# Stacked keys and values fetched as 120 and 8 partition rows, and w3's last ternary step ahead of two maxima

## What is computed

```python
x = x + xattn0(layernorm(x), ctx, mask)            # softmax(x ctx^T / sqrt(512)) ctx
x = x + ffn0(layernorm(x), w1, w2, w3)             # ternary weights, inputs rounded to 8 bits
x = x + xattn1(layernorm(x), ctx, mask, Wq, Wk, Wv, Wo, ...)   # 16 heads of 32
x = x + ffn1(layernorm(x), integer weights and scales)

def weight_quant(w):                               # w1, w2, w3 of ffn0
    scale = 1.0 / clip(mean(abs(w)), EPS)
    return clip(round(w * scale), -1, 1) / scale
```

## Time and profile before

| | us |
|---|---|
| median of 3 runs | 488.27 (486.84 to 489.53) |
| the profiled execution's own time | 488.89 |
| its span | 487.2 |
| granted TensorE clock over the span | 0.993 |

### The profile page before, as it was taken

How to read it: one execution, slowest core, us unless ns; L and a number is a source line. 1 busy time by engine, 2 the same in 40 slices (tenths; PEclk the granted TensorE clock), 3 DMA queues, 4 the chain that set the end, 5 groups by cost and what they waited for, 6 DMA issues and landing times.

```text
span 487.2 us, 10104 instructions
## 1 busy us (share of the span) xinstructions
PE 467.1 (96%) x3942; PEld 355.4 (73%) x3951; DVE 294.4 (60%) x557; ACT 235.4 (48%) x362; POOL 83.3 (17%) x105
## 2 busy tenths in 40 slices
PE   8999999999999899999999688989999999999997
PEld 6877788777877566676798566878886665556996
DVE  4964464458857887655755323777885976555111
ACT  4655433553576365463846545957755492222000
POOL 2210400005024000001071011232332252000000
PEclk9999999999999999999999988999999999999999
DMA  8999787923694145233397977867323452000111
GB/s 274 352 337 358 288 286 237 314 87 126 229 293 132 54 112 149 70 90 77 104 303 216 267 230 283 245 234 240 110 59 119 131 170 68 1 0 0 39 57 57
DMA packets 59181, 82.75 MB, mean 170 GB/s; under 512 B 20097, under 2 KB 43649, under 8 KB 57985
## 3 DMA queue, kind: packets, MB, share of 16 engines
q1 hardware_dynamic: 59136, 82.14, 53.5%
q10 hardware_dynamic: 2, 0.01, 0.0%
HBM read 58.76 MB, written 14.42 MB: 150 GB/s over the span
## 4 chain that ended last, share of the span: by engine, by line
PE 88%; DVE 7%; issue 3%; DMA 1%; ACT 1%; POOL 0%; DVEq 0%; ACTq 0%
PE psum L1536 14%; PE psum L189 13%; PE psum L187 13%; PE psum L1586 7%; PE psum L1377 6%; PE psum L1339 4%; PE psum L652 4%; PE psum L1444 4%; PE psum L1491 4%; PE psum L1322 4%; PE psum L1386 3%; PE psum L1494 3%; PE psum L1474 3%; PE psum L1503 2%; DVE e L1870 1%
## 5 line engine op out<-in xcount | busy, mean ns | idle before, releaser
L189 PE MATMUL psum<-wv_p,kv_p 128*128 128x512 f32 x288 | 76.2, 413 | 0.0
L187 PE MATMUL psum<-kv_p,wk_p 128*128 128x384 f32 x384 | 74.2, 343 | 0.0
L187 PEld LDWEIGHTS psum<-kv_p,wk_p 128*128 128x128 f32 x384 | 66.8, 188 | 2.1 <-issue 0.2
L189 PEld LDWEIGHTS psum<-wv_p,kv_p 128*128 128x128 f32 x288 | 53.7, 188 | 15.8 <-issue 3.7
L1202 ACT ACTIVATE e<-psum,mask_bias 128x448 f32<-128x448 f32 x96 | 53.9, 637 | 22.7 <-PE psum L1474 22.4
L1870 DVE TENSOR_SCALAR e<-e 128x1344 f32<-128x1344 f32 x32 | 28.8, 900 | 20.1 <-ACT e L1202 20.1
L1491 PE MATMUL psum<-e,vst 128*32 128x112 f32 x768 | 38.2, 270 | 1.6 <-issue 0.9
L1536 PE MATMUL psum<-xt,wg_b 128*128 128x448 f16 x176 | 36.9, 352 | 0.3 <-issue 0.3
L1536 PE MATMUL psum<-xt,wu_b 128*128 128x448 f16 x176 | 36.9, 352 | 0.0
L1586 PE MATMUL psum<-h_p,wd_r 128*128 x176 | 36.7, 369 | 0.0
L209 DVE SCALAR_TENSOR_TENSOR khl<-psum,bqk,khl 128x384 f16<-128x384 f32 x32 | 19.6, 613 | 27.0 <-ACT khl L199 26.8
(11 more groups left out here) (188 smaller groups left out, 815.8 us busy)
## 6 DMA issues: line engine op xcount, KB each, us to landing
kst<-k_scratch SPq DMA_DIRECT2D x32, 384.0 KB, 6.4
kv_raw<-in_ctx_feat SPq DMA_DIRECT2D x12, 768.0 KB, 5.8
w_stage<-in_w SPq DMA_DIRECT2D x6, 1408.0 KB, 8.0
cn<-in_ctx_tok SPq DMA_DIRECT2D x8, 768.0 KB, 9.6
k_scratch<-khl SPq DMA_DIRECT2D x128, 48.0 KB, 1.9
v_scratch<-vsp SPq DMA_DIRECT2D x24, 256.0 KB, 2.8
vst<-v_scratch SPq DMA_DIRECT2D x8, 768.0 KB, 4.6
qst<-qhl SPq DMA_DIRECT2D x32, 112.0 KB, 4.7
```

The lines of the kernel that those rows point to most:

```text
L187: mm = pe.matmul(psum[:, kv_bank(p), 0:TP], wk_p[:, u, k, n * P:(n + 1) * P], src[:, v, k, :], **ends)
L189: mm = pe.matmul(psum[:, kv_bank(p), :], src[:, u, k, n * P:(n + 1) * P], wv_p[:, v, k, :], **ends)
```

## The change

Two things. Each fetch of stacked keys and of stacked values becomes two DMAs on the same queue, one for partitions 0 to 119 and one for 120 to 127, and the two waits count twice as many. Of the source of the keys the slices are 60 and 4 rows, each of which is read twice. Nothing else of SP's order moves. And on DVE `ternary_weight(dve, 2, 1)` and then `hidden(1, 1, 2)` move ahead of the two `largest_input`.

```diff
+        ROWS = ((0, 120), (120, P))
+
         def keys_fetch(sp, b, g):
-            sp.dma_start(kst[b % 2][:, g].rearrange("p h t -> p (h t)"),
-                         k_scratch[b, :, :, g].rearrange("u d h (o t) -> (u d) o (h t)", o=1)
-                         .to_broadcast([2 * HD, 2, 4 * TP])).then_inc(kst_loaded[b % 2], 16)
+            src = k_scratch[b, :, :, g].rearrange("u d h (o t) -> (u d) o (h t)", o=1)
+            for lo, hi in ROWS:
+                sp.dma_start(kst[b % 2][lo:hi, g].rearrange("p h t -> p (h t)"),
+                             src[lo // 2:hi // 2].to_broadcast([(hi - lo) // 2, 2, 4 * TP])).then_inc(kst_loaded[b % 2], 16)

         def values_fetch(sp, b, q):
-            sp.dma_start(vst[q][:], v_scratch[b]).then_inc(vst_loaded[q], 16)
+            for lo, hi in ROWS:
+                sp.dma_start(vst[q][lo:hi], v_scratch[b, lo:hi]).then_inc(vst_loaded[q], 16)
...
-                    pe.wait_ge(kst_loaded[b % 2], 16 * G * (b // 2 + 1))
+                    pe.wait_ge(kst_loaded[b % 2], 16 * G * len(ROWS) * (b // 2 + 1))
...
-                    pe.wait_ge(vst_loaded[b % 2], 16 * (b // 2 + 1))
+                    pe.wait_ge(vst_loaded[b % 2], 16 * len(ROWS) * (b // 2 + 1))
...
             gate_scales(2, 0)
+            ternary_weight(dve, 2, 1)
+            hidden(1, 1, 2)
             largest_input(dve, 5)
             largest_input(dve, 6)
-            hidden(1, 1, 2)
-            ternary_weight(dve, 2, 1)
             input_scales(dve, 1)
```

## The result

The changed kernel takes **508.3 us** (median; 505.7 to 511.3), the kernel before 487.6 (486.1 to 489.5): a ratio of **1.043, 95% interval 1.038 to 1.048**, slower by some 21 us. The forecast was 479.4 with a range of 476.5 to 491, so the sign was wrong and the time lies outside the range. The profiled execution took 507.0 us, its span is 505.3.

The account below looks back on a forecast made before the run. PE, busy 96% of the span, was taken as the bound, its late idle time as waits for its program: 488.9 - 0.85 + 2.1 - 8.5 - 2.3 + 0.6 = 479.9, forecast 479.4 us at the median, range 476.5 to 491.

Parts of the forecast that it names:

- The stalls: Second attention: PE's five waits for its program, 10.3 us, mostly vanish once one engine carries no keys or values; -8.5 us.
- the free engine: Key and value fetches: 120 rows use 15 engines, and the one left out brings PE's program sooner; chance 0.46.
- The clock: Second attention: PE's half-clock stretches after two long stalls mostly go, 2.3 of 2.5 us; -2.3 us.
- SP's issues: Ahead of the attention: 8 more key issues, 5.1 us, make first scores 0.6 late and values 2.1 in all; +2.1 us.
- Fuller engines: Keys of b = 2: a fetch ends with its fullest engine, 10 rows instead of 8, 1.25 us against 1.0; +0.6 us.
- w3: Before down(0): the last ternary step ends 1.71 us earlier, PE's 1.51 us stall goes, part returns at gate_up; -0.85 us.
- Rival 3: Second attention: program fetch shares an engine that gets the 8 rows on top, stalls lengthen, +3.5, 493 us; chance 0.18.

Follow-up runs that it names:

- e12_120_8_late: Kernel before with key and value fetches split at row 120 from the third batch on, the first two batches whole; ratio 1.0211.
- e13_120_8_early: Kernel before with key and value fetches split at row 120 in the first two batches alone, later ones whole; ratio 1.0126.
- e8_120_alone: Kernel before, fetching only rows 0 to 119 of keys and values from the third batch on, with no second transfer; ratio 1.0276.
- e3_96_32: Kernel before with each key and value fetch cut into 96 and 32 rows, DVE's order unchanged; ratio 1.0242.
- e1_w3_only: Kernel before with only the new order on DVE, no fetch split; ratio 0.9985.
- e7_columns: Kernel before with each fetch cut in two along the row (keys by heads, values by chunks), every transfer of 128 rows; ratio 0.9992.
- e9b_paced: Kernel before with SP holding fetches back until earlier ones have landed, no transfer changing its shape; ratio 1.026.

## Why the prediction was wrong

**The step that failed** is in "The stalls": "A transfer of 128 rows can be laid on 16 engines in equal parts of 8 rows, one of 120 rows only on 15", and then a price for rows (ten instead of eight take 1.25 us) that takes a packet's time as given. The layout was right: 94.5% of 16 engines, and 152 packets more than before. By the rule of the Trainium skill, page "DMA: Bandwidth & Descriptors", section "Why a DMA increments its semaphore by 16 and not by 1" (15 engines for 120 rows, 4 and 8 for the 8 rows), there are 32 x (15 + 4 - 16) + 8 x (15 + 8 - 16) = 152 more closing packets, so the measurement agrees with that rule to the packet. What was wrong is that a packet of the same row takes 0.19 us instead of 0.13. That term was in neither the sum nor a rival. Over the 60 us from 280 on it makes 69 us of engine time for a megabyte out of 49, in a stretch where the DMA share was already 0.76. From the third batch on this costs 10 of the 21 us (`e12_120_8_late`); the first two batches, where slow packets and SP's longer issues act together, cost 6 (`e13_120_8_early`).

**The stalls**, predicted at -8.5 us, became longer and more: 23.6 us of "issue" with the first scores' 3.7 in it, against 10.3. What the prediction read them as holds up: each of 20 stalls in three traces ends 1.3 to 1.6 us after a packet of the program, in after they stand 127 or 128 matmuls or twice that apart, and with a bounded queue the first three were 0.7 to 0.8 us. What failed is the step from there to the free engine, that the packet would stand there behind stacks, Wo and integer weights alone: `e8_120_alone` has a free engine, program packets that start as late as in before, and stalls of up to 3.6 us. Whether the packet uses another engine, or waits for something else that a loaded queue delays, no run here tells apart. The prediction also read the DMA share of the stretches as 0.80 to 1.06 from two of the four; the one before the fourth stall (287.89 to 299.97 us) has 0.66.

**The clock**, predicted at -2.3, went the other way as well. After has more stretches at the lower level of 1.2 GHz behind its stalls: of four windows of 3 us, that after the stall of 338.28 has PEclk 0.50, those after 283.7 and 300.1 0.65 and 0.76, and that after 309.7, where PE had stood still for 2.93 us, 1.00. PE's busy time is 5.1 us longer in all.

**SP's issues** were right in kind and half of the size. Predicted: 8 more issues of 0.64, first scores 0.6 late, +2.1 for the values. The queue of SP in after:

```profile
242.41 12.73 SPq L243 DMA_DIRECT2D kst<-k_scratch  x16
255.46 10.32 SPq L544 DMA_DIRECT2D qst<-qhl  x16
265.82 2.60 SPq L248 DMA_DIRECT2D vst<-v_scratch  x4
```

```profile
L243 SPq DMA_DIRECT2D kst<-k_scratch x64: 630/847/1868, 242.4 to 352.4; - x64
```

The key issues take 12.73 us against 6.62, 6.1 more instead of 5.1, and the stacks start 4.2 us later instead of 2.3. The last line (duration in ns, min/median/max) has the cause: one by one, the issues alternate between 0.85 us for 120 rows and 0.63 for 8. In `e3_96_32` the median of the 64 is 598 ns. "0.59 us whether it has 16 or 112 rows" was read from moves of `xres`, and does not hold for 120 rows of keys. To this came slower landing: the last keys and the stacks share the queue, and a stack landed in 3.8 us (2.6 in the earlier trace rows). `e13_120_8_early` prices the whole start at 6.1 us (4.0 to 8.3), three times the term, with slow packets in it.

**Fuller engines**, +0.6, is the term in which most of the loss should have stood. It was worked out from 10 rows in place of 8; that part is not seen, as the 8-row transfers cost nothing that shows in `e12_120_8_late`.

**w3**, -0.85, was right in its mechanism: no idle time stands before `down(0)` in after, and some appears at the next `gate_up`. It gives back 1.1 us in after and 1.3 in `e1_w3_only`, not 0.65, so what is left is 0.2 to 0.4 in PE's waits, and 0.7 with an interval of -0.9 to 2.3 in the time.

**The rivals.** Rival 3 had the sign and named the wrong mechanism; its 493 counts an engine with ten rows, and `e3_96_32`, with all engines even, shows that evenness doesn't help. The rival that was missing is "a transfer that doesn't span 128 rows is slower on every engine". The trace of before had a hint that I did not weigh: the query stacks, written 64 rows at a time, run at a DMA share of 0.72 and 185 GB/s (253.5 to 256 us), 62 us of engine time for a megabyte, where keys of 128 rows take 43 (379 GB/s at 1.015). Their packets are smaller, 1792 bytes. By the same view one takes 0.719 x 16 x 2.5 / 257 = 0.11 us, where the 1536 bytes of `e7_columns` take 0.07, so size is not all of it. But they come from SBUF and not from DRAM, which no run separates.

## What to carry to other kernels

Before a transfer is cut, ask along which axis: cutting it across the partitions made every packet of it slower here, cutting it within the row did not (1.024 to 1.044 against 0.999 for the same number of transfers). In a trace, divide the DMA share by the rate over a loaded stretch; if engine time for a byte rises while the bytes stay, look for a layout and not for a count. And a freed engine is worth nothing before it is known that the waiting work uses it. Where an engine stands still on "issue" within a run of one kind, look for the packet of its program just ahead of the end.

## What was not expected of the hardware

- The same row of 3072 bytes takes an engine 0.13 us in a fetch of 128 rows, 0.19 to 0.20 in fetches of 120, 96/32 or 64/64 rows, and 0.25 when only rows 0 to 63 are written. The mechanism is not shown.
- SP needs 0.60 us to issue a key fetch whether it has 128 rows or 96 and 32, but 0.85 for one of 120 rows.
- 40 more transfers of whole 128-row layout cost nothing measurable (0.9992), though each adds 16 small packets and 0.6 us of SP.
- PE's stalls within runs of one kind end 1.3 to 1.6 us after a packet of its program does, in before, after and `e8_120_alone`. They are 0.9 to 2.9 us long in before, up to 4.5 in the change, and 0.7 to 0.8 for the first three in `e9b_paced`.
